# Graph attention and expert layer on one core: the plan stays in SBUF, preparations run beside the gathers, and TensorE's and VectorE's instructions of an item stand in another order

## What is computed

```python
n = layernorm(x)                                # without weights
ft = (n @ W).reshape(N, 4, 64)                  # 4 heads
e  = leaky(e_src[src] + e_dst[dst])             # slope 0.2, e_* = sum(ft * w_att_*)
ex = exp(e - emax[dst]);  a = ex / denom[dst] * dist
x  = x + segment_sum(ft[src] * a, dst)
x  = x + top2_of_6_experts(layernorm(x))        # router 256-128-6, experts 256-256-256-256
```

## Time and profile before

| what | us |
|---|---|
| median of 3 runs (3122.08 to 3132.09) | 3129.61 |
| the profiled execution | 3125.72 |
| its span, first to last instruction | 3124.0 |
| busy in the span: TensorE, VectorE, ScalarE, GpSimd | 2332.9, 1824.0, 1467.0, 2095.2 |
| mean granted clock of TensorE | 0.869 |
| first gather of main's rows starts | 186.92 |
| first instruction of the experts block | 2304.97 |

### The profile page before, as it was taken

The page is one execution under the profiler, slowest core; times in us unless marked ns, Lnnn a source line. Parts: engine busy times, 40 slices in busy tenths (PEclk is TensorE's granted clock), DMA queues, the critical chain, the costliest instruction groups (busy, mean ns, idle before and its releaser), DMA issues. The chain is left out here.

```text
span 3124.0 us, 62545 instructions
## 1 busy us (share of the span) xinstructions
PE 2332.9 (75%) x15568; PEld 1888.6 (60%) x15569; DVE 1824.0 (58%) x4215; ACT 1467.0 (47%) x2676; POOL 2095.2 (67%) x2064
## 2 busy tenths in 40 slices
PE   4946667767777777777777777777739999899995
PEld 3725555555556555666565666656637877777774
DVE  6855444555566666677777777777769333332232
ACT  2513223334444454455555666556625554444442
POOL 0046777777777777777777776666406777777775
PEclk9966777877878888889989998988869999999997
DMA  5645555555655666666666656555550445455443
GB/s 173 193 120 152 161 159 163 173 171 168 175 173 173 177 180 176 184 188 183 191 183 178 186 179 182 169 171 163 136 95 9 82 79 81 77 81 83 79 77 46
DMA packets 231876, 450.52 MB, mean 144 GB/s; under 512 B 55818, under 2 KB 148782, under 8 KB 230769
## 3 DMA queue, kind: packets, MB, share of 16 engines
q0 software_dynamic: 114816, 265.53, 36.5%
q1 hardware_dynamic: 76616, 140.14, 14.1%
q10 hardware_dynamic: 39924, 38.86, 3.8%
HBM read 376.74 MB, written 69.01 MB: 143 GB/s over the span
## 5 line engine op out<-in xcount | busy, mean ns | idle before, releaser
L422 POOL DMA_INDIRECT rows<-table,src_col x1568 | 1505.2, 960 | 559.8 <-issue 460.9
L1376 PE MATMUL m_A<-m_msg,m_by_edge 128*128 128x260 f32 x3920 | 1169.1, 461 | 262.6 <-issue 194.0
L1376 PEld LDWEIGHTS m_A<-m_msg,m_by_edge 128*128 128x128 f32 x3920 | 888.6, 233 | 455.7 <-issue 263.7
L1230 ACT ACTIVATE m_apart<-drow,nid 128x1024 bf16 x297 | 341.0, 1148 | 654.1 <-SPq L963 577.2
L1064 DVE TENSOR_TENSOR m_msg<-rows,m_A 128x2048 f32<-128x2048 f32 (+1 forms) x294 | 568.0, 1932 | 111.4 <-issue 103.4
L1584 POOL DMA_INDIRECT out<-x_con,x_to_i x206 | 329.2, 1598 | 105.8 <-issue 79.8
L1362 PEld LDWEIGHTS m_E<-m_look_parts,m_by_node 128*128 128x128 bf16 x7104 | 231.6, 97 | 271.0 <-issue 234.2
L1362 PE MATMUL m_E<-m_look_parts,m_by_node 128*128 x7104 | 245.3, 167 | 187.6 <-ACT m_by_node L1233 180.8
L1040 DVE TENSOR_TENSOR m_z<-m_E,rows 128x64 f32<-128x64 f32 x295 | 65.7, 223 | 486.2 <-PE m_E L1362 363.1
L1233 ACT ACTIVATE m_by_node<-m_apart,m_one 128x1024 bf16<-128x1024 bf16 x297 | 341.0, 1148 | 9.7
L1026 DVE TENSOR_TENSOR m_by_edge<-m_A,row 128x1024 f32<-128x1024 f32 (+1 forms) x295 | 306.8, 1040 | 0.4 <-issue 0.2
(11 more groups left out here) (246 smaller groups left out, 2257.3 us busy)
## 6 DMA issues: line engine op xcount, KB each, us to landing
drow<-edges SPq DMA_DIRECT2D x196, 512.0 KB
rows<-table,src_col POOLq DMA_INDIRECT x1568
table<-f_rowbuf SPq DMA_DIRECT2D x14, 924.0 KB, 4.9
ydram<-m_y ACTq DMA_DIRECT2D x49, 264.0 KB
m_xb<-in_x ACTq DMA_DIRECT2D x48, 256.0 KB
out<-m_x ACTq DMA_DIRECT2D x48, 256.0 KB
f_xin<-in_x SPq DMA_DIRECT2D x13, 896.0 KB, 7.0
x_w<-in_L_ffn_expert_w SPq DMA_DIRECT2D x18, 256.0 KB, 5.7
```

Of the source, the lines that this page charges most:

```text
L422: nc.gpsimd.indirect_dma_start(K.rows[:, g % RING, j, :], None, table, bass.IndirectOffsetOnAxis(ap=K.src_col[:, g, j:j + 1], axis=0)).the ...
L1230: a.activation(apart[i][:, :], drow[:, bass.ds(g % RING, 1), :].rearrange("p a n -> p (a n)"), ACT.Abs, bias=K.nid[:, bass.ds(b, 1)], scal ...
L1376: m = t.matmul(psA[i][:, 0:MSG], by_edge[i][:, j, :], msg[i][:, j, :], start=(j == tiles[0]), stop=(j == tiles[-1]))
```

## The change

- The plan is one integer tile `K.plan` in SBUF from edge_tables on. GpSimd clears it; VectorE writes the integers straight into it. The float table, its clearing and its cast, the store to DRAM, the wait for it and the read back are gone.
- SP no longer waits for the last stores of `table` at the end of features; GpSimd waits for them ahead of its first gather. `rowbuf` therefore lives on through the early blocks, and `xn` borrows the place of the ring.
- `split_look` runs at the end of lookup_table, beside the gathers of group 2; `sums` is cleared there by ScalarE.
- TensorE in item k: the pair's work (turn, router or score) first, then `look_up(k + 2)`, `sum_up(k)`, and then the fetch of the next words.
- VectorE in item k: the branch on the half (two nested branches for the half cases, with fixed tiles) stands ahead of `add_score`, `wd` and the product; `slope_score(k + 1)` comes behind the product. READY and DUE are loaded in item 0 ahead of `add_sums`; the branch on DUE sits inside the one on a complete pair.

```diff
@@ -308,7 +309,23 @@
+def split_look(v, st, K):
+
+    rest = K.look_rest[:, :, :]
+    ends, bound = K.look[:, :, 0:HEADS], K.look[:, :, HEADS:2 * HEADS]
+    st.did(v.scalar_tensor_tensor(rest[:, :, 0:HEADS], ends, SLOPE, bound, ALU.mult, ALU.subtract))
+    st.did(v.tensor_tensor(rest[:, :, HEADS:2 * HEADS], ends, bound, ALU.subtract))
+    st.settle()
+    for n in range(3):
+        part = K.look_parts[:, :, 8 * n:8 * n + 8]
+        st.did(v.tensor_copy(part, rest))
+        st.settle()
+        if n < 2:
+            st.did(v.tensor_tensor(rest, rest, part, ALU.subtract))
+            st.settle()
...
@@ -467,15 +484,15 @@
...
-            sp.wait_ge(asked, 6)
-            sp.dma_start(sched, tab_i[:, :]).then_inc(stored, 16)
-            sp.wait_ge(stored, 16)
...
         def _(pool):
             nc.gpsimd.iota(blk_i[:, :], [[P, NBD]], base=0, channel_multiplier=0).then_inc(consts, 1)
             nc.gpsimd.iota(kk_i[:, :], [[1, 320]], base=0, channel_multiplier=0).then_inc(consts, 1)
             nc.gpsimd.iota(brow_i[:, :], [[1, 1]], base=0, channel_multiplier=1).then_inc(consts, 1)
+            nc.gpsimd.memset(plan[:, :], 0).then_inc(consts, 1)
+            for h in range(2):
+                pool.wait_ge(K.table_stored[h], 16 * (NQ // 2))
             pool.wait_ge(copied, 4)
             for g in range(AHEAD - 1):
                 gather(nc, K, table, g)
@@ -518,7 +535,6 @@
...
-            st.did(v.memset(tab[:, :], 0.0))
@@ -590,26 +606,25 @@
...
+            dve.wait_ge(consts, 4)
+
             def column(at, words, i, of):
-                st.did(v.tensor_copy(tab[:, at + i:at + words * NW:words], of))
...
+                st.did(v.tensor_copy(plan[:, at + i:at + words * NW:words], of))
+
+            st.did(v.memset(plan[:, SUMS_AT:SUMS_AT + 1], NB))
+            st.did(v.tensor_copy(plan[:, SUMS_AT + 4:SUMS_AT + 4 * NW:4], flat[:, 0:NW - 1]))
...
-            st.did(v.tensor_copy(tab[:, REL + RING:REL + NG], rel[:, 0:NG - RING]))
-            st.settle()
-            st.did(v.tensor_copy(tab_i[:, :], tab[:, :]))
-            st.settle()
-            v.nop().then_inc(asked, 1)
+            st.did(v.tensor_copy(plan[:, READY + 1:READY + 2 * NCH], pairs[:, 0:2 * NCH - 1]))
+            st.did(v.tensor_scalar(plan[:, DUE + 1:DUE + NIT], pairs[:, 0:NIT - 1], -float(WAITING), 0.0, ALU.add, ALU.max))
+            st.did(v.tensor_copy(plan[:, REL + RING:REL + NG], rel[:, 0:NG - RING]))
...
@@ -621,15 +636,23 @@
...
         @block.gpsimd
         def _(pool):
             gather(nc, K, table, AHEAD - 1)
+
+        @block.scalar
+        def _(act):
+            act.wait_ge(zeroed, 1)
+            nc.scalar.activation(K.sums[:, :, :], zero[:, :].unsqueeze(2).broadcast_to([P, AR, MSG]), ACT.Copy)\
+              .then_inc(cleared, 1)
+            act.wait_ge(cleared, 1)
...
@@ -736,8 +761,9 @@
...
-        xn = [sb(f"xn{h}", [P, HB, D]) for h in range(2)]
-        rowbuf = [sb(f"rowbuf{h}", [P, HB, ROW]) for h in range(2)]
+        flat = K.rows[:, :, :, :].rearrange("p r a n -> p (r a n)")
+        xn = [flat[:, h * HB * D:(h + 1) * HB * D].rearrange("p (b d) -> p b d", b=HB) for h in range(2)]
+        rowbuf, stored = K.rowbuf, K.table_stored
...
@@ -792,8 +817,6 @@
...
             store(2 * LAST + 1, 1, LAST)
-            for h in range(2):
-                sp.wait_ge(stored[h], 16 * (LAST + 1))
             sp.wait_ge(K.edge.stored, 16)
...
@@ -1044,22 +1060,19 @@
...
-            def item(k, i):
-
-
+            def item(k, i, between=None):
...
                 after = (i + 1) % 3
-                add_score(k + 1, after)
-                group, rws = rows_of(i)
-                dve.wait_ge(exped, k + 1)
-                v.tensor_tensor(wd[i], msg[i][:, :, D:MSG], flat(K.dist_col[:, bass.ds(group, 1), :])
-                                .unsqueeze(2).broadcast_to([P, GT, HEADS]), ALU.mult).then_inc(wd_made, 1)
-                slope_score(k + 1, after)
                 only = dve.snap(words[i][3], min_val=0, max_val=GT)
 
-                def multiply(tiles, n):
+                def weigh(tiles, n):
+                    add_score(k + 1, after)
+                    group, rws = rows_of(i)
+                    dve.wait_ge(exped, k + 1)
+                    v.tensor_tensor(wd[i], msg[i][:, :, D:MSG], flat(K.dist_col[:, bass.ds(group, 1), :])
+                                    .unsqueeze(2).broadcast_to([P, GT, HEADS]), ALU.mult).then_inc(wd_made, 1)
                     dve.wait_ge(wd_made, k + 1)
...
@@ -1068,12 +1081,18 @@
...
                 with dve.If(only == GT):
-                    multiply(slice(0, GT), GT)
+                    weigh(slice(0, GT), GT)
                 with dve.Else():
-                    multiply(bass.ds(dve.snap(words[i][3], min_val=0, max_val=HALF), HALF), HALF)
+                    with dve.If(only == 0):
+                        weigh(slice(0, HALF), HALF)
+                    with dve.Else():
+                        weigh(slice(HALF, GT), HALF)
+                slope_score(k + 1, after)
                 before = dve.snap(words[i][0], min_val=0, max_val=NB)
                 keep_block(after)
                 fetch((i + 2) % 3, k + 2)
+                if between:
+                    between()
                 add_sums(k, before, after)
                 edge_onehot(k + 1, after)
...
@@ -1135,29 +1154,14 @@
...
-            v.memset(sums[:, :, :], 0.0).then_inc(ready, 1)
             v.memset(y[:, :, D:YW], 0.0).then_inc(ready, 1)
...
             v.tensor_scalar(less_base[:, :], K.base[:, :], -1.0, None, ALU.mult).then_inc(ready, 1)
 
-            st = Steps(dve, look_steps)
-            rest = look_rest[:, :, :]
-            ends, bound = K.look[:, :, 0:HEADS], K.look[:, :, HEADS:2 * HEADS]
...
-            dve.wait_ge(ready, 5)
+            dve.wait_ge(ready, 4)
 
             v.nop().then_inc(added, 1)
-            dve.wait_ge(plan_in, 16)
             fetch(0, 0)
...
@@ -1169,26 +1173,28 @@
...
                     it = lap * TURNS + turn_of_lap
+                    def plan_of_turn():
+                        dve.load([ready_pairs], plan[0:1, bass.ds(it + READY, 1)])
+                        dve.load([due_pairs], plan[0:1, bass.ds(it + DUE, 1)])
+                        dve.reg_alu(due_now, due_pairs, 0, ALU.max)
+
                     for i in range(HI):
-                        item(it * HI + i, i)
+                        item(it * HI + i, i, plan_of_turn if i == 0 else None)
                         if i == 0:
-                            dve.load([ready_pairs], plan[0:1, bass.ds(it + READY, 1)])
                             ready_now = dve.snap(ready_pairs, min_val=0, max_val=NPAIR)
                             with dve.If(dve.snap(done, min_val=0, max_val=NPAIR) < ready_now):
                                 take_sums(index(done), it * HI + 2)
-                        if i == 2:
-                            with dve.If(dve.snap(done, min_val=0, max_val=NPAIR) < ready_now):
-                                normalize(index(done))
-                                dve.reg_mov(done, index(done) + 1)
-                    now = dve.snap(done, min_val=0, max_val=NPAIR)
-                    dve.load([due_pairs], plan[0:1, bass.ds(it + DUE, 1)])
-                    dve.reg_alu(due_now, due_pairs, 0, ALU.max)
-                    due = dve.snap(due_now, min_val=0, max_val=NPAIR)
-                    with dve.If(now < due):
-                        with dve.Fori(now, due) as pair:
-                            take_sums(dve.snap(pair, min_val=0, max_val=NPAIR - 1), it * HI + 4)
-                            normalize(dve.snap(pair, min_val=0, max_val=NPAIR - 1))
-                        dve.reg_mov(done, due)
+
+                    with dve.If(dve.snap(done, min_val=0, max_val=NPAIR) < ready_now):
+                        normalize(index(done))
+                        dve.reg_mov(done, index(done) + 1)
+                        now = dve.snap(done, min_val=0, max_val=NPAIR)
+                        due = dve.snap(due_now, min_val=0, max_val=NPAIR)
+                        with dve.If(now < due):
+                            with dve.Fori(now, due) as pair:
+                                take_sums(dve.snap(pair, min_val=0, max_val=NPAIR - 1), it * HI + 4)
+                                normalize(dve.snap(pair, min_val=0, max_val=NPAIR - 1))
+                            dve.reg_mov(done, due)
...
@@ -1408,15 +1413,12 @@
...
-            pe.wait_ge(ready, 1)
 
             t.nop().then_inc(summed, 1)
             for i in (1, 2):
                 t.matmul(psA[i][:, 0:MSG], sums[:, 0, 0:P], sums[:, 0, :], start=True, stop=True).then_inc(summed, 1)
             t.nop().then_inc(y_turned, 1)
             t.nop().then_inc(lg_copied, 1)
-            pe.wait_ge(plan_in, 16)
-            pe.wait_ge(look_steps, 7)
             pe.wait_ge(weights_in, 16 * ROUTER_LOADS)
...
@@ -1430,9 +1432,6 @@
...
                     for i in range(HI):
                         k = it * HI + i
```

(29 more changed lines are left out.)

63 lines of the change are left out of this document (16 added, 47 removed).

## The result

| | before | changed |
|---|---|---|
| median of 4 runs each | 3125.85 us | **3181.11 us** |
| ratio, 95% interval | | 1.0178 [1.0161, 1.0194] |
| span of the profiled execution | 3124.0 us | 3182.5 us |
| TensorE's granted clock in it, mean | 0.869 | 0.850 |

The change makes the kernel 55 us slower; the forecast was 60 us faster. A control, the same kernel again (e5), gave 1.0168 [1.0146, 1.0191] at a clock of 0.854.

What follows compares the result with a forecast made beforehand. GpSimd's gather pace was taken to bound the kernel to 1650 us, VectorE's stream of items behind it. From 3125.7, -10 for the start and -54 for the items gave 3061.7, as a median 3065 us; 8-in-10 range 3032 to 3103.

Steps and rivals of the forecast that it cites:

- (a): End of the features block: SP's wait for the table stores moves to GpSimd, beside the making of src_col; -3.8 us.
- (e): Main block's start: clearing and the plan's way back leave, but ScalarE's one-hots wait behind a load of x; -2.7 us.
- (b): Ahead of the first gather: the float table's clearing leaves VectorE, GpSimd clears the plan instead at no cost; -2.1 us.
- (c): Block end behind GpSimd's last gather: the cast, the store and its wait no longer keep it open; -1.9 us.
- (d): lookup_table: the split of the look-up table moves behind VectorE's work there, beside 8 gathers; +1.5 us.
- (f): VectorE's items: with the half's branch moved, idle time ahead of the product goes, -0.46 us; some returns ahead of scores, +0.1.
- second rival: The branches only change their place: a half case jumps twice, little gain is left in the items; 3100 us, chance 0.2.
- (g): VectorE's items: loads of READY and DUE run beside the product, halving the idle time ahead of the scores; -0.25 us.
- (h): slope_score behind the product starts ScalarE later; normalize waits 0.8 us in 24 turns with a pair; +0.2 us an item.
- (i): TensorE's items: the fetch behind the sums is hidden by queued matmuls, so VectorE's wait for look-ups shrinks; -0.1 us.
- third rival: TensorE's look-ups and sums wait for ScalarE's copy_turned, and its clock falls; slower, 3142 us, chance 0.06.

Runs made afterwards that it cites:

- e5: The changed kernel again without any edit, as a control; 3182.74 us, 1.0168 of the kernel before.
- e16: The kernel e13 with GpSimd's clearing of the plan moved to the first block; 0.9852 of the kernel before, in a set where that takes 4086 us.
- e7: The changed kernel with slope_score ahead of the product again, as in the kernel before; 3121.77 us, 0.9987 of the kernel before.
- e8: The changed kernel with slope_score ahead of the product and TensorE's order of the kernel before; 3122.97 us, 0.9986 of the kernel before.
- e13: e12 with two copies of VectorE's item code in place of three, the half taken from a register; 3113.46 us, 0.9957 of the kernel before.
- e12: e9 with VectorE's loads of READY and DUE back where the kernel before had them; 3120.93 us, 0.9982 of the kernel before.
- e9: The changed kernel with slope_score ahead of the product and TensorE's look-ups before the pair's work, fetch still behind the sums; 3117.95 us, 0.9973 of the kernel before.
- e11: e7 with 111 more VectorE instructions in a never-taken branch at the end of the loop; 3139.30 us, 1.0039 of the kernel before.
- e6: The changed kernel with TensorE's order of the kernel before (look-ups, fetch, pair's work, sums), slope_score still late; 3171.36 us, 1.0146 of the kernel before.

## Why the prediction was wrong

**What bounds it.** Right that VectorE's stream is the chain behind GpSimd's pace. Wrong that this begins at 1650 us whatever the change does: with dearer items the takeover comes earlier. The changed kernel's 145th addition, at about 1365 us, still comes 6.3 us earlier than that of the kernel before; the 151 behind it lose 59.8 us. So each tenth of a us an item counts some 150 times, not 104.

**The start, (a) to (e), -10 us: -4.1.** Of the difference 2.0 us is spread: in this execution the features block ended at 174.45 for 172.47 (ScalarE's last instruction), while other executions with the same code up to there end it between 172.3 and 174.2. Counted from that end the start gave 6.1. The failed step is (b): -2.1 was forecast, and from GpSimd's first instruction of the block to the first gather it takes 8.6 us for 8.0 (6.5 in e16). GpSimd's clearing was taken as free beside VectorE's casts; it is not, because the casts wait for it (2.4 us each, 0.2 and 0.3 in e16, whose clearing lies far ahead). "Were it 3 times as dear, the first gather would come 2 us later" guarded against a slow clearing, while it took 2.40 us, as estimated, and cost that through its neighbour. The forecast had the Trainium skill, "SBUF — State Buffer", section on the two separate sides, at hand for VectorE's copies beside gathers. There the trace agrees with the forecast and not with the full lock: beside the split gathers take up to 1.71 us for 0.95, and an operation of the split 0.98. The 4.9 us that the forecast worked out from that rule are also too many, since it speaks of copies, and of the five operations only the three casts (2.9 us) are such. (a) gave 3.2 us, the gap behind ScalarE's last instruction of the features block being 3.3 for 6.5. (c) and (d) came to -0.1 for -0.4. From main's first gather to the first freed slot it takes 14.3 us for 17.7, so (e) was right in size, 3.4 for 2.7, though only half of it lies ahead of the one-hots.

**(f), -0.46 us an item: right at its place, nothing in sum.** The idle time ahead of the product went, and came back ahead of the scores and the additions (92.6 us before, 104.9 in e7). This is the second rival, "the branches only change their place", and e7 and e8 give what it says of (f). Its price for the rest, 3100, was still 20 us too low. So none of the 37 us that (f) was to give showed in e7. Part of it is the branch of the third copy: from the start of a half product to the addition, in the second and third items of a turn, the median is 1.27 us before, 1.45 in e7 and 1.27 in e13. **(g)**, -0.25, had the wrong sign. In the kernel before, READY is loaded while the one-hot runs; now the two loads stand between a product and the addition, and behind a half product of 1.22 us nothing hides them. From the start of a half product to the addition it takes 1.27 us in the mean before, 1.74 in e7, 1.39 in e12 with the loads back, and 1.29 in e13. In time e12 and e9, which differ by these loads, are alike (3120.93 and 3117.95), so what e12 gains there it gives back elsewhere.

**(h), +0.2 us an item: the step that made the loss.** The mechanism was right, and so was the size of its one part: `normalize` waits 17.7 / 22 = 0.8 us in a turn with a pair, as forecast. Two parts were missing. With `slope_score` early its 0.18 us lies in the gap between the small product `wd` and the large one, which has to be waited out in any case; behind the product it lies on the stream, which the forecast put at nothing. The medians from the start of the product to the addition are 2.44 and 1.58 us in the changed kernel and 2.34 and 1.49 in e7, full and half: 0.1 us an item. And no term held the loop's jump back, which costs 2.8 us in the mean from there on with three copies and the late `slope_score`, and 0.6 in e7. Between the 145th addition and the last, the changed kernel takes 976.0 us and e7 916.3. Of these 59.7 us, 15.4 are jumps (19.5 - 4.1), 21.0 waits of `normalize` for ScalarE (23.2 - 2.2), and 0.1 x 150 = 15 the place of `slope_score` itself. About 8 us stay unexplained, and so does why the load behind the jump starts late.

On that jump the forecast named the Trainium skill, "Runtime: NRT & Kernel Launch", section "Instruction fetch mechanics": a taken branch out of the fetched window stalls until its target is there. The trace agrees as far as e11 shows it: only code that never runs was added, and the jump went from 0.5 to 2.3 to 3.9 us. The loads fit it too: where the jump is dear, one starts about when the branch is taken or later, and VectorE goes on 1.8 to 2.3 us after its start. The forecast applied the rule to the short jumps inside an item, where a half item pays 0.18 us for the third copy, and not to the one long jump of the loop. The profile's row of instructions loaded, of the kernel before (packets, MB, share):

```profile
q14 instruction: 307, 2.51, 0.3%
```

And of the changed kernel, the same in e7:

```profile
q14 instruction: 349, 2.86, 0.3%
```

42 loads of 8 KB more; e13, with two copies, has 321. As e7 has 349 too, their number does not make the jump dear.

**(i), -0.1 us: too small to see.** It would be 10 us; e9, which differs from e8 by the fetch alone, is 5 us faster, and the intervals overlap.

**The third rival** (TensorE waits for ScalarE ahead of its look-ups) had the right sign for the wrong reason. The waits are there, 23.6 us in 16, longest 2.8, and the clock falls. But e7 has them too, 16.1 us in 13, longest 3.1, and runs at 0.9987; and e6, where they are 6.7 us in 9, still runs at 1.0146. Both signs that the forecast named for being wrong came: items over 6 us behind 1850 with renamed gaps, and these waits. The second turned out to point at the wrong cause.

**The sum.** Forecast -10 and -54. For e7 the traces show -4 to -6 and about 0, and it measures about -5; the late `slope_score`, with the jump that goes with it, adds 60. No case of the forecast put the price there.

## What to carry to other kernels

Before a small instruction is moved "out of the way", look at what it stands in now: one that fills a gap between two dependent instructions costs nothing, and anywhere else it can lengthen the stream (here 0.1 us of its 0.18) and delays whoever waits for it. Idle time called issue belongs to the sequencer's stream of loads and branches, so moving a branch moves the gap; count what stands between two long instructions, and whether the shorter form of the work still hides it. Look at the jump back of an unrolled loop as well, since a loop can pay there for instructions that it never runs.

## What the runs showed of the hardware

- 111 instructions that are never run cost 17.5 us in a loop of 14 laps (e11 against e7), nearly all of it at the jumps back. Where the jump was dear, VectorE went on 1.8 to 2.3 us after the start of an 8 KB load of instructions that started up to 1.9 us behind the branch; where it took 0.5 us in e7, that load had started 2.3 to 4.0 us ahead.
- Casts of int32 to float32 on VectorE, 0.2 and 0.3 us long, took 2.4 us each beside a memset of GpSimd of 2.40 us (changed kernel against e16), and ended 0.1 and 0.2 us behind it, while operations of the split slowed a gather only from 0.95 to 1.5 to 1.7 us.
- The same kernel before took 3126 to 3131 us in some sets and 4030 to 4086 in others, on the same chip number among them. In the latter, TensorE's look-ups were issued one by one with gaps of 1.2 to 2 us while gathers ran. The cause stays open.
- A lower granted clock of TensorE (0.860 for 0.875, e7 and e8) came with no difference in the time (3121.77 and 3122.97 us), while VectorE set the pace.
